# A decoder layer's feed-forward: rows split in two parts, kept in DRAM or split again

## The reference, cut to what matters

```python
x = act_qdq(x)                                # round to int16 steps, one scale
up = act_qdq(x @ lpbq_dequant(w_up).T)        # 256 -> 768
gate = act_qdq(x @ lpbq_dequant(w_gate).T)    # 256 -> 768
sig = fixed_qdq_u16(jax.nn.sigmoid(gate))
gate = act_qdq(gate * sig)
o = act_qdq(gate * up)
return o @ lpbq_dequant(w_down).T             # 768 -> 256
```

## Time and profile before

| what | value |
|---|---|
| median of 3 runs | 1506.33 us (1505.71 to 1507.38) |
| profiled execution, its own time | 1508.49 us |
| its span, first to last instruction | 1506.7 us |
| mean granted TensorE clock | 0.937 |
| busy over the span: PE, DVE, ACT, POOL | 86%, 71%, 62%, 22% |
| from 1200 to 1250 us (gate): PE, DVE, ACT, POOL | 50.00, 29.22, 29.62, 0.35 us of 50 |
| from 1250 to 1300 us (sigmoid and up): PE, DVE, ACT, POOL | 44.50, 45.85, 43.72, 34.35 us of 50 |
| from 1300 to 1350 us: PE, DVE, ACT, POOL | 21.87, 49.83, 26.70, 11.36 us of 50 |

### The profile page before, as it was taken

One profiled execution on the slowest core, in us unless ns is written; L12 is line 12 of the kernel. 1 busy time (PEld: TensorE's weight loads), 2 busy tenths in 40 slices (PEclk: granted clock), 3 DMA queues, 4 the chain that ended last, 5 costly groups with the idle time before them and its releaser, 6 DMA issues. The chain is left out here.

```text
span 1506.7 us, 24880 instructions
## 1 busy us (share of the span) xinstructions
PE 1295.7 (86%) x8220; PEld 689.7 (46%) x8220; DVE 1067.8 (71%) x2582; ACT 940.3 (62%) x1649; POOL 335.6 (22%) x577
## 2 busy tenths in 40 slices
PE   5857799999999999999999999987996898820497
PEld 2423333443343344334334433435885687610486
DVE  4335688778878878887887888852564468999655
ACT  2322377777777777777777777671675659749600
POOL 2422211212112121211212121003462005600012
PEclk9988899999999999999999999997998899965699
DMA  3999769778786977878697786327321002316032
GB/s 103 269 288 308 207 195 260 208 224 217 220 222 193 259 215 213 223 212 225 201 256 212 210 230 185 106 75 228 97 72 43 15 1 107 133 48 243 0 100 96
DMA packets 260415, 260.61 MB, mean 173 GB/s; under 512 B 65822, under 2 KB 246718, under 8 KB 256190
## 3 DMA queue, kind: packets, MB, share of 16 engines
q1 hardware_dynamic: 260286, 259.02, 59.6%
HBM read 147.46 MB, written 110.71 MB: 171 GB/s over the span
## 5 line engine op out<-in xcount | busy, mean ns | idle before, releaser
L540 ACT ACTIVATE pr<-scoresT 128x512 f32<-128x512 f32 x1024 | 550.5, 600 | 218.6 <-PE scoresT L791 159.9
L787 PE MATMUL scoresT<-qT,kT 99*128 99x512 bf16 (+7 forms) x1408 | 359.3, 326 | 6.9 <-DMA qT<-sh 5.3
L642 DVE TENSOR_REDUCE mx<-scores_for_max 128x1 f32<-128x888 f32 (+6 forms) x448 | 301.6, 673 | 0.0
L637 DVE CUSTOM_DVE_ANT_0 junk<-scores_for_max,win 128x200 f32<-128x200 f32 (+2 forms) x512 | 180.0, 352 | 162.5 <-PE scores_for_max L762 155.0
L640 DVE TENSOR_REDUCE mx<-scores_for_max 128x1 f32<-128x64 f32 (+6 forms) x448 | 277.5, 619 | 0.0
L804 PE MATMUL attn_out<-pr,vS 128*17 128x512 f32 x2048 | 269.5, 598 | 0.1
L787 PEld LDWEIGHTS scoresT<-qT,kT 99*128 99x128 bf16 (+1 forms) x1408 | 114.0, 97 | 335.5 <-ACT rows L520 97.8
L791 PE MATMUL scoresT<-idf,win 128*128 128x128 f32 x1024 | 218.7, 275 | 0.0
L437 POOL COPY rows<-rows 128x736 f32<-128x736 f32 x128 | 102.1, 799 | 400.0 <-ACT rows L520 400.0
L761 PE MATMUL scores_for_max<-kX,qT 64*128 64x512 bf16 x512 | 165.0, 384 | 11.0 <-DVE mx L642 9.3
L762 PE MATMUL scores_for_max<-kX,qX 64*128 64x512 bf16 x512 | 165.0, 384 | 0.0
(11 more groups left out here) (194 smaller groups left out, 1797.6 us busy)
## 6 DMA issues: line engine op xcount, KB each, us to landing
rel_table<-rows SPq DMA_DIRECT2D x128, 512.0 KB, 4.3
win<-rel_table SPq DMA_DIRECT2D x128, 512.0 KB, 5.4
up_raw<-xT_normed SPq DMA_DIRECT2D x6, 1536.0 KB, 5.1
xT_normed<-up_raw SPq DMA_DIRECT2D x6, 1536.0 KB, 6.5
qT<-q_parts SPq DMA_DIRECT2D x32, 256.0 KB, 7.5
kX<-k_parts SPq DMA_DIRECT2D x64, 128.0 KB, 4.8
kT<-k_parts SPq DMA_DIRECT2D x32, 256.0 KB, 5.4
q_parts<-part SPq DMA_DIRECT2D x32, 192.0 KB, 5.7
```

Of the source, the lines that this page charges most:

```text
L540: nc.scalar.activation(pr[:, n % NPR, h, :], bank, ACT.Exp).then_inc(t_read, 1)
L637: last = nc.vector.tensor_tensor_reduce(junk[:, n % 2, 0:z - a], bank[:, a:z], win[:, T % NW, q4, h, u:u + z - a], 1.0, NEG, ALU.add, ALU. ...
L642: last = nc.vector.tensor_reduce(mx[:, T % 2, q4, h, 2:3], bank[:, z:L], AX.X, ALU.max)
L787: last = mm(bank[:, a:e], k[0:r], q[0:r, a:e], start=(n == 0), stop=not near and n == len(pieces) - 1, skip_group_check=True)
```

## The change

While the gate is computed, SP stores both parts of blocks 0 to 5 in a new DRAM tensor `xd`, as soon as DVE has made them (`f_xg`); `split_rows` waits, for n >= 2, until the slot's last content has been stored (`x_st`). For up block j >= 2 SP loads both parts back into the slot (`load_parts`), once PE is through with block j-2; PE waits for these loads (`x_ld`) in place of POOL. In SP's queue the loads of block j+3 stand ahead of the store of up block j, and the wait ahead of the loads of `second_norm` falls away. `split_again`, its three semaphores and its scratch tile go.

```diff
--- before.py
+++ after.py
@@ -846,6 +846,7 @@
 
     h2d = nc.dram_tensor("second_norm", [NBLK, HALF, D], F32, kind="Internal").ap()
     ud = nc.dram_tensor("up_raw", [NBLK, P, FT * HALF], F32, kind="Internal").ap()
+    xd = nc.dram_tensor("x_parts", [NBLK - 2, 2, P, 2 * HALF], F32, kind="Internal").ap()
 
     with ExitStack() as ctx:
         def sb(name, shape, dt=F32):
@@ -949,7 +950,7 @@
         cross_attention(nc, sem, ad, x, ident, woT, bo, ctxT, xwq, xwkT, xwvT, xbq, xbk, xbv, wdq,
                         h2d, idf, wuh, wul, wgh, wgl, wdT, xr, neg_half, magic, s_half, amax, top_all, ps, l_sum, l_rstd,
                         norm_stats, norm_rstd, norm_scalar, largest_of, scale_of, scale_pool)
-        feed_forward(nc, sem, spare, h2d, ud, wgh, wgl, wuh, wul, wdT, xr, ps, magic, coarse, step, inv, t_inv, amax,
+        feed_forward(nc, sem, spare, h2d, ud, xd, wgh, wgl, wuh, wul, wdT, xr, ps, magic, coarse, step, inv, t_inv, amax,
                      largest_of, scale_of, scale_pool, l_sum, norm_stats, norm_rstd, norm_apply, out)
 
 
@@ -1484,7 +1485,7 @@
                 turn_x(n)
 
 
-def feed_forward(nc, sem, spare, h2d, ud, wgh, wgl, wuh, wul, wdT, xr, ps, magic, coarse, step, inv, t_inv, amax,
+def feed_forward(nc, sem, spare, h2d, ud, xd, wgh, wgl, wuh, wul, wdT, xr, ps, magic, coarse, step, inv, t_inv, amax,
                  largest_of, scale_of, scale_pool, l_sum, norm_stats, norm_rstd, norm_apply, out):
 
     M_ALL = FT * NBLK
@@ -1521,16 +1522,14 @@
         ub = [old[:, j * FT * HALF:(j + 1) * FT * HALF] for j in range(2)]
         gi = [gi0[:], old[:, 2 * FT * HALF:2 * FT * HALF + FT * HALF // 2].bitcast(I16)]
         ui = [si[:].bitcast(I16), old_int[:, 0:FT * HALF]]
-        x_one = old[:, 2 * FT * HALF + FT * HALF // 2:]
         work = ub
         res = [old_int[:, (4 + 2 * j) * 2 * HALF:(6 + 2 * j) * 2 * HALF].bitcast(F32).rearrange("p (q d) -> p q d", d=D) for j in range(2)]
 
         f_xi = sem("f_xi")
         f_xh = sem("f_xh")
         f_xg = sem("f_xg")
-        f_x1 = sem("f_x1")
-        f_x2 = sem("f_x2")
-        f_xu = sem("f_xu")
+        x_st = [sem(f"x_st{j}") for j in range(2)]
+        x_ld = [sem(f"x_ld{j}") for j in range(2)]
         f_full = sem("f_full")
         f_out = sem("f_out")
         f_gmax = sem("f_gmax")
@@ -1564,10 +1563,27 @@
 
         @block.sync
         def _(sp):
+            def whole(t, n):
+                return t[:, n % 2].bitcast(F32).rearrange("p c n -> p (c n)")
+
+            def load_parts(j):
+                n = UP[j]
+                sp.wait_ge(f_full, M_ALL + FT * (j - 1))
+                for k, t in enumerate((xh, xl)):
+                    sp.dma_start(whole(t, n), xd[n, k]).then_inc(x_ld[n % 2], 16)
+
+            for n in range(NBLK - 2):
+                sp.wait_ge(f_xg, n + 1)
+                for k, t in enumerate((xh, xl)):
+                    sp.dma_start(xd[n, k], whole(t, n)).then_inc(x_st[n % 2], 16)
+            for j in range(2):
+                sp.wait_ge(x_st[j], 16 * (NBLK - 2))
+            load_parts(2)
             for j in range(NBLK - 2):
+                if j + 3 < NBLK:
+                    load_parts(j + 3)
                 sp.wait_ge(f_out, M_ALL + FT * (j + 1))
                 sp.dma_start(ud[j], ub[j % 2]).then_inc(u_st[j % 2], 16)
-            sp.wait_ge(f_xu, 2 * (NBLK - 2))
             for n in range(2):
                 sp.dma_start(res[n], rows_of(h2d, n)).then_inc(o_ld[n], 16)
             for j in range(NBLK - 2):
@@ -1590,23 +1606,7 @@
 
         @block.gpsimd
         def _(pool):
-            def split_again(j):
-
-                n = UP[j]
-                pool.wait_ge(f_full, M_ALL + FT * (j - 1))
-                for c in range(2):
-                    k = 2 * (j - 2) + c
-                    if k:
-                        pool.wait_ge(f_xu, k)
-                    nc.gpsimd.tensor_copy(x_one, xi[:, c, n, :]).then_inc(f_x1, 1)
-                    pool.wait_ge(f_x1, k + 1)
-                    nc.gpsimd.tensor_copy(xh[:, n % 2, c], x_one).then_inc(f_x2, 1)
-                    pool.wait_ge(f_x2, k + 1)
-                    nc.gpsimd.tensor_tensor(xl[:, n % 2, c], x_one, xh[:, n % 2, c].bitcast(F32), ALU.subtract).then_inc(f_xu, 1)
-
             scale_pool(pool, 1)
-            for j in range(2, NBLK):
-                split_again(j)
             scale_pool(pool, 2)
             scale_pool(pool, 3)
             scale_pool(pool, 4)
@@ -1693,6 +1693,7 @@
                 dve.wait_ge(f_xi, n + 1)
                 if n >= 2:
                     dve.wait_ge(f_full, FT * (n - 1))
+                    dve.wait_ge(x_st[n % 2], 32 * (n // 2))
                 nc.vector.tensor_copy(xh[:, n % 2], xi[:, :, n, :]).then_inc(f_xh, 1)
                 dve.wait_ge(f_xh, n + 1)
                 nc.vector.tensor_tensor(xl[:, n % 2], xi[:, :, n, :], xh[:, n % 2].bitcast(F32), ALU.subtract).then_inc(f_xg, 1)
@@ -1808,7 +1809,7 @@
                 project(FT * n, n, wgh, wgl, early=n == 0)
             for j in range(NBLK):
                 if j >= 2:
-                    pe.wait_ge(f_xu, 2 * (j - 1))
+                    pe.wait_ge(x_ld[UP[j] % 2], 32 * (j // 2))
                 project(M_ALL + FT * j, UP[j], wuh, wul)
             pe.wait_ge(f_out, 2 * M_ALL)
 
```

## The result

The changed kernel takes 1503.64 us (median of 20 runs, 1501.27 to 1507.63), the kernel before 1506.81 us in 20 runs beside it (1502.51 to 1511.02). The ratio is 0.9982 with a 95% interval of 0.9973 to 0.9990: faster, by 2.7 us (1.5 to 4.1). The forecast of 3.8 us, a ratio of 0.9975, lies inside the interval. Whether the gain is over or under 0.2% is not settled by it. The profiled execution took 1503.47 us, its span is 1501.7 us, 5.0 less than the span before.

A forecast was written before the change was run, and what follows sets the result against it. The prediction took DVE to bound the sigmoid stretch, held up by POOL's splitting. Its terms, 0 (gate) - 3.8 (DVE) + 0 (loads) + 0 (moved store), took 1506.33 to 1502.5 us, range 1501.0 to 1505.8.

The forecast's parts named there:

- The main term: Sigmoid stretch of seven turns: without POOL's splitting, DVE's steps and products run clean, 3.8 us less.
- the rival that DVE's excess has another cause: Sigmoid stretch: DVE's excess does not come from POOL and stays, time 1506.3 us; chance 0.06.
- The gate's stretch: Twelve added stores of 512 KB and waits ahead of six DVE splits while the gate is computed: 0 us.
- The loads: Up stretch: twelve loads of 512 KB, PE waiting on them instead of POOL; a pair takes 6.8 to 8.1, costing 0.
- The nearest row: Earlier profile's row for two loads issued together behind a store, 6.8 to 8.1 us, used for the up stretch's pairs.
- the estimate: Traffic in a turn of 11.58 us: 2.62 MB, 226 GB/s, against about 358 GB/s for a core.
- The moved store: Store of up block j behind the loads of block j+3: 0 us expected; as a rival that decides, chance 0.03.
- the cover: Third up block on ACT: 5.3 us of slack against a slot at worst 3.2 us late.
- The slower side: Rival: loads bound PE, or gate stores take over 15 us a pair; 1517.5 us at L = 20; chance 0.06.
- My formula: PE needs (8.24 + L) / 2 for a block with load time L; DVE's 11.58 stays the bound until L = 14.9.
- the first case: The forecast itself holds, 1502.5 us, faster by over 0.2%, own range 1501.5 to 1503.3; chance 0.72.

The follow-up runs named there:

- the one in which POOL works for nobody: Changed kernel plus POOL's 36 old instructions on a scratch tile that nobody uses: ratio 1.0000 to the kernel before, seven turns 82.32 us.
- the halved instructions: Kernel before with each of POOL's 36 instructions cut into two of 256 columns: ratio 0.9980, seven turns 81.45 us.
- the fills: Changed kernel plus POOL filling a 128x512 scratch tile ten times for each of six blocks: ratio 0.9984 to the kernel before, seven turns 81.52 us.
- two equal programs: Kernel before measured once more as a kernel of its own, nothing changed: ratio 0.9993, seven turns 84.88 against 84.91 us.

## Why the prediction was right, and where it was not

- **The main term.** 84.99 - 7 x 11.58 - 0.09 = 3.84 was the forecast; 3.82 is measured, and each further kernel with POOL silent in this stretch and its feeds in time has 81.08 or 81.09. Against the rival that DVE's excess has another cause stand five such profiles, and the one in which POOL works for nobody and 1.23 come back. That is a third of the 3.82; the whole is accounted for by the six stretched instructions of the kernel before, each matched with what POOL had under way. One argument of the forecast is misworded: a stretched DVE instruction does not end as POOL's does (the one of 1266.58 ends at 1269.42, POOL's at 1267.80); what matches is its extra time and the rest of POOL's. That it is a wait and not shared bandwidth is shown by the halved instructions and by the fills, which touch line 1738 and not 1740.
- **The gate's stretch.** Nothing was forecast. Stores land in 2.6 to 4.4 (2.6 for the first and 3.6 for the second of a pair in the median), no split waits for one, and without them the stage is 0.1 us shorter.
- **The loads.** I gave a pair 6.8 to 8.1 in the up stretch; the first of a pair lands in 3.5 to 4.3 and the second in 4.4 to 6.1. The nearest row was too slow by about 2 us, on the safe side. It is of loads in pieces of 1 KB, issued behind a store, and these are in pieces of 4 KB; which of the two makes the difference was not tested. PE waits for none, though the DMAs move 254 GB/s from 1255 to 1310, more than the 226 of the estimate.
- **The moved store.** I allowed 5.1 alone and up to 13.2 behind a pair; 6.3 to 9.7 is what it takes. ACT's third up block begins at 1271.80 with no wait, so the cover was not used.
- **The slower side.** It was the right mechanism with a wrong price: at loads released 8.24 later, PE is the bound, but the bound is (load + 8.24 + 2.3), where the 2.3 is what the lower clock after each wait costs. My formula, 15 us for L = 20, left this out. In the changed kernel itself no wait of PE brings it into play.
- **The chances.** The step that was too sure is the last: 0.72 for faster by over 0.2%. The forecast lay 0.05% beyond that line, while an interval here is 0.1% to each side, and two equal programs came out 0.07% apart. The two measurements of the changed kernel, 0.18% and 0.23%, lie on both sides of it. The median, 1503.64, is inside the range of 1501.0 to 1505.8, but above the 1501.5 to 1503.3 that the first case was given for itself: it is the stage, not the whole time, that bears the forecast out. The spread isn't in the changed stage. The first split starts anywhere from 1172.0 to 1177.3 us over the profiles of this study, in code that all share, from there to the first largest up value it is 83.8 to 85.4 where POOL has no part in the first block, and the first down products are 12.0 to 13.5, by when the granted clock rises.

## What to carry to other kernels

POOL can slow a DVE-bound stage from off the critical path: look for DVE instructions of one form with uneven durations, and lay POOL's timeline beside them. The cost is set by what POOL has under way when DVE arrives, so shorter POOL instructions, or a place beside one-input reductions or in a stage that DVE does not bound, can recover most of it without moving the data. Cutting POOL's instructions in half got 3.5 of the 3.8 us with no transfer at all, in one phase of the two engines; another phase may give less. Where a stage has stable durations, forecast and measure that stage; a gain of 0.25% can't be told from 0.2% by whole times that spread over 0.4 to 0.6%.

## What the runs showed of the hardware beyond that

- The first subtraction of POOL came 7.0 us after it was free before, 7.0 to 8.9 in the experiments that have one, with no instruction at work in between; later ones follow at once.
- POOL's multiplication from float to 16-bit steps took 7.95 us for 3072 columns and 5.36 for 2048, more than twice the price per column of its casts (0.61 for 512).
- A wait of PE of some 6.5 us ahead of each block of 36 matmuls made the block 10.5 us long in place of 8.24.
